# Two-layer transformer kernel: the causal mask of layer two's key-major scores moves from TensorE products to a VectorE minimum behind the exponentials, with a new order of all five engines

## What is computed

```python
xn = _layernorm(x, axis=-1)
x = x + _L1_attn_ref(xn, ...) + _L1_ffn_ref(xn, ...)      # 16 heads; 32 experts, top 6, and a shared expert

c = ...                                    # per head: keys in a latent of 64, normalised
scores = jnp.einsum('bhsl,bhtl->bhst', q_lat, c) * (1.0 / np.sqrt(L))
mask = jnp.tril(jnp.ones((Sx, Sx), dtype=bool))
scores = jnp.where(mask, scores, -jnp.inf)
w = jax.nn.softmax(scores, axis=-1)
oh = jnp.einsum('bhst,bhtd->bhsd', w, v)
```

## Time and profile before

| | |
|---|---|
| median of 3 runs | 2020.04 us (2015.65 to 2021.65) |
| profiled execution: device time | 2017.58 us |
| its span, first to last instruction | 2015.8 us |
| mean granted TensorE clock | 0.976 of full speed |
| TensorE busy | 1746.5 us, 87% |
| VectorE, GpSimd, ScalarE busy | 1100.9, 874.7, 819.5 us |
| one body, in the middle of the program | 116.2 us |

### The profile page before, as it was taken

One profiled execution on the slowest core, in us unless ns is written; L12 is line 12 of the kernel. 1 busy time (PEld: TensorE's weight loads), 2 busy tenths in 40 slices (PEclk: granted clock), 3 DMA queues, 4 the chain that ended last, 5 costly groups with the idle time before them and its releaser, 6 DMA issues.

```text
span 2015.8 us, 41842 instructions
## 1 busy us (share of the span) xinstructions
PE 1746.5 (87%) x16112; PEld 1333.6 (66%) x16112; DVE 1100.9 (55%) x2557; ACT 819.5 (41%) x1596; POOL 874.7 (43%) x995
## 2 busy tenths in 40 slices
PE   3657898989999998989989898999989899888887
PEld 2434676767677676767767676776767677675766
DVE  5645373655647365664737465473746547364442
ACT  2532435344343534334353433435353443534332
POOL 2312343535354454435444353534535353543455
PEclk7878999999999999999999999999999999999999
DMA  5632222313142231314132141413213141321221
GB/s 129 163 85 62 59 59 64 81 43 87 37 102 53 74 73 51 76 40 105 47 83 64 51 87 36 107 37 91 56 53 85 37 107 37 93 54 46 54 64 33
DMA packets 323318, 139.26 MB, mean 69 GB/s; under 512 B 227568, under 2 KB 308528, under 8 KB 323120
## 3 DMA queue, kind: packets, MB, share of 16 engines
q1 hardware_dynamic: 304688, 86.23, 18.5%
q0 software_dynamic: 18432, 50.36, 9.1%
HBM read 102.12 MB, written 29.88 MB: 65 GB/s over the span
## 4 chain that ended last, share of the span: by engine, by line
PE 26%; issue 25%; DVE 19%; POOL 17%; ACT 8%; SPq 3%; DMA 2%; POOLq 0%; DVEq 0%; ACTq 0%
PE s3r L1394 7%; POOL gs L762 6%; POOL h2l L771 5%; POOL cb L741 3%; PE s2acc L1391 3%; DVE th L1269 3%; DVE mx L1102 3%; PE s1a L1394 2%; DVE gs L1274 2%; PE s2r L1394 2%; PE s1acc L1497 2%; POOL h1p L706 2%; PE s1a L1514 2%; ACT h2h L967 1%; ACT p L876 1%
## 5 line engine op out<-in xcount | busy, mean ns | idle before, releaser
L771 POOL TENSOR_TENSOR h2l<-th,h2h 128x512 f16<-128x512 f32 (+1 forms) x224 | 246.5, 1103 | 390.9 <-ACT h2h L967 380.5
L762 POOL TENSOR_TENSOR gs<-gs,cb 128x512 f32<-128x512 f32 x192 | 243.9, 1270 | 263.6 <-DVE gs L1274 262.2
L967 ACT CAST h2h<-th 128x512 f16<-128x512 f32 (+1 forms) x224 | 131.2, 586 | 425.8 <-DVE th L1269 356.9
L1394 PE MATMUL s3r<-xe,xg 128*128 128x256 f16 x2304 | 284.5, 273 | 2.7 <-DVE gs L1274 2.7
L1391 PE MATMUL s2acc<-xd,h2h 128*128 128x256 f16 x1536 | 263.9, 274 | 24.5 <-POOL h2l L771 24.5
L1394 PE MATMUL s3r<-xe,xu 128*128 128x256 f16 x2304 | 283.0, 273 | 1.6 <-DVE th L1269 1.6
L1394 PEld LDWEIGHTS s3r<-xe,xg 128*128 128x128 f16 x2304 | 222.7, 98 | 39.9 <-DVE gs L1274 8.7
L1394 PEld LDWEIGHTS s3r<-xe,xu 128*128 128x128 f16 x2304 | 223.7, 98 | 31.6 <-DVE th L1269 5.5
L741 POOL DMA_DIRECT2D cb<-comb_d x384 | 229.0, 604 | 20.9 <-issue 11.2
L1274 DVE SCALAR_TENSOR_TENSOR gs<-th,s3r 128x512 f32<-128x512 f32 (+1 forms) x224 | 143.9, 642 | 148.8 <-ACT th L971 148.4
L1269 DVE TENSOR_TENSOR th<-s3r,gs 128x512 f32<-128x512 f32 x192 | 132.1, 688 | 168.5 <-POOL gs L762 164.5
(11 more groups left out here) (280 smaller groups left out, 3140.4 us busy)
## 6 DMA issues: line engine op xcount, KB each, us to landing
cb<-comb_d POOLq DMA_DIRECT2D x128, 192.0 KB, 3.4
part_d<-part SPq DMA_DIRECT2D x32, 512.0 KB, 3.3
cb<-comb_d POOLq DMA_DIRECT2D x128, 128.0 KB, 3.0
stacks<-part_d SPq DMA_DIRECT2D x192, 64.0 KB, 2.4
va<-v_d SPq DMA_DIRECT2D x512, 8.0 KB
cb<-comb_d POOLq DMA_DIRECT2D x128, 64.0 KB, 3.0
land<-part_d SPq DMA_DIRECT2D x96, 64.0 KB, 2.7
part<-part_d SPq DMA_DIRECT2D x96, 64.0 KB, 3.5
```

The source lines that it names most:

```text
L762: g.tensor_tensor(gc2[:, p % 2, :], gs2[:, p % 2, :], cb2[:, 2 * (p % 6):2 * (p % 6) + 2, :].rearrange("p a s -> p (a s)"), ALU.mult).then ...
L771: g.tensor_tensor(h2l[0:m, n % 2, 0:w], th2[0:m, n % 2, 0:w], h2h[0:m, n % 2, 0:w], ALU.subtract).then_inc(sem("h2l_made"), 1)
L967: s.copy(h2h[0:m, n % 2, 0:w], th2[0:m, n % 2, 0:w]).then_inc(sem("h2h_made"), 1)
L1394: ins = nc.tensor.matmul(bk, lhs[i][k], rhs[j][k], start=first, stop=last)
```

## The change

Three things:

1. The mask product of the key-major scores of layer two (old L1655, `mm(two(ring2[u % 2])[:, :, 0:P], identb, maskk1, ...)`) goes: 16 per sequence. The second score product of each head now ends the group and signals ScalarE. Entries above the diagonal go through the exponential unmasked.
2. VectorE gets one instruction per pair of heads (new L1242): a minimum, in place in p, of the two diagonal blocks of both heads (128 partitions by 4 x 128, fp32) with a table `keep1` (broadcast), which is 1e30 where the entry stays and 0 where it goes. It waits until the exponential of the pair's second head is done and signals `p2_masked`. `weigh` of four heads now waits for `p2_masked` of its second pair in place of the last exponential.
3. All 25 order strings are replaced (one each is shown).

```diff
@@ ORDERS @@
     "pe": {
-        "body": ("022020012122001121002101022221120220212100142212101012131301200103100101031101310120001003"
-                 "34300300403040003043343303001333133"),
+        "body": ("220020102010222101201021102241221022120202100121211112130132020101031100001100113033101003"
+                 "04300300403040003433041030333333031"),
...
@@
-        maskk1 = sb("maskk1", [P, P], BF16)
+        keep1 = sb("keep1", [P, P])
@@ def dve2 @@
+                dve.wait_ge(*emptied2(it, U2["k_rows", 2 * n + 1]))
+                diagonal = p1[:, :, :, :].rearrange("p s k (c q) -> p s (k c) q", q=P)[:, 2 * n % PSLOT:2 * n % PSLOT + 2, 0:3:2, :]
+                v.tensor_tensor(diagonal, diagonal, keep1[:, :].unsqueeze(1).unsqueeze(1).to_broadcast([P, 2, T, P]),
+                                ALU.min).then_inc(sem("p2_masked"), 1)
                 yield
@@
-            v.tensor_scalar(maskk1[:, :], mask_tmp[3], -BIG, None, ALU.add).then_inc(sem("dve_const"), 1)
+            v.tensor_copy(keep1[:, :], mask_tmp[3]).then_inc(sem("dve_const"), 1)
@@ def pe2, weigh @@
-                pe.wait_ge(*emptied2(it, U2["k_rows", QUAD * q + QUAD - 1]))
+                pe.wait_ge(*event("p2_masked", it, 2 * q + 2))
@@ def pe2 @@
-                        mm(ring2[u % 2][:, at:at + S - P * j], key(kst2, h, FULL)[:, P * j:P * j + P],
-                           query(qst2, h, FULL)[:, P * j:S], start=j == 0, stop=False, skip_group_check=True)
-                for u, h in pair:
-                    mm(two(ring2[u % 2])[:, :, 0:P], identb[:, :], maskk1[:, :].unsqueeze(1).to_broadcast([P, T, P]),
-                       start=False, stop=True, skip_group_check=True).then_inc(fills2(u), 1)
+                        ins = mm(ring2[u % 2][:, at:at + S - P * j], key(kst2, h, FULL)[:, P * j:P * j + P],
+                                 query(qst2, h, FULL)[:, P * j:S], start=j == 0, stop=j == T - 1, skip_group_check=True)
+                        if j == T - 1:
+                            ins.then_inc(fills2(u), 1)
```

More of the change, by code:

```diff
@@ new lines @@
+        "start": ("022200213010031120000002001213010300230101230000103112101410110020203034023111211143002020"
+                 "10234031010242341032330231133021231"),
+        "first": ("010002001310100113203211003032033223123101231131110023311212301023000103200043302100011110"
+                 "24040302400022012104214300322112000"),
+        "late": ("002001212110122011022201241112402221201221120002001312001203311321121002003301000040311300"
+                 "03110013003330433043043000330013031"),
@@ new lines @@
+        "start": ("001000020021003000110020200002020120121103011000413320113121230120131343031102333103211022"
+                 "24331020410101230104322012142333010"),
+        "first": ("104001002111022100312212300130100000020101011221301112012001133121311010213103202033231304"
+                 "20130022300401220400004300333343202"),
+        "late": ("202200120122200112110242120212140202221022121113121013003211030010320110103141031101030030"
+                 "10000300340030030040000103333413333"),
@@ new lines @@
+        "start": ("210002200110112010122010301000010000011222102000131030421100031032031234203332014340302010"
+                 "13212330000223124131023343321111010"),
+        "first": ("010011202021210010311020302001301000011112001232212213010310201111001231011323410331334001"
+                 "03002213202040000004300223323423034"),
+        "late": ("020210201212010212214201241202102022222114211011220132031301104320003011103101041311001300"
+                 "00030300030000030003100043133313333"),
@@ new lines @@
+        "start": ("220011201222000001003100010022111110102100120000102030001300310423214002213002240201400201"
+                 "31343101131023100322241313333313331"),
+        "first": ("120010100202121321000211102300030113132012120110000012210123001111113101321300402300123303"
+                 "41030002243020420021040033240303233"),
+        "late": ("002120010442212010202121201212142201111224222201031231100101313003011102103001312100013020"
+                 "01030003000300330000031433031033343"),
```

72 lines of the change are left out of this document (24 added, 48 removed), and 2 rows, old and new, of the table PER.

## The result

| | before | after |
|---|---|---|
| median | 2020.85 us (2015.65 to 2022.02, 4 runs) | 2099.74 us (2098.14 to 2104.04, 4 runs) |
| ratio to before, 95% interval | | 1.0398, 1.0381 to 1.0416 |
| one body, middle of the program | 116.21 us | 122.29 us |
| TensorE busy, whole program | 1746.5 us | 1753.0 us |
| mean granted TensorE clock | 0.976 | 0.959 |

The change costs 79 us, 4%. The prediction was 2008 us with a range to 2040: wrong in sign and 60 us outside the range.

A forecast was written before the change was run, and what follows sets the result against it. TensorE, busy 87% of the span, bounds the kernel. Per period -1.76 (masks) + 0 (A) + 1.4 (R) + 1.2 (P) - 1.4 (C) = -0.56 us, taken as -0.75, -12 us in all: 2008 us, range 1988 to 2040.

The forecast's parts named there:

- Nothing hides these products: Mask products: each pair costs TensorE's queue 0.22 us, 1.76 us per sequence, 28 us in all if idle time stays.
- rival 2: Nothing gained: the freed 1.76 us reappear as waits in R and P, set by SyncE and VectorE; 2014 to 2026 us, chance 0.18.
- The minimum, 0.65 us: VectorE: each of eight minima per sequence takes 0.65 us, 5.2 us per period, fitting into its idle time.
- the collision term: Minima on VectorE excluded by GpSimd instructions: 0.2 to 1 us per period, mostly in idle time, put at nothing.
- stretch A: Transpose of the maxima through key-major heads to the last value product's end: 23.74 us before, idle time forecast unchanged within 0.1.
- 0.9, 0.25 and 0.65 us: New waits in A from VectorE's queue, at the second and third value products and behind the first eight heads' normalising.
- C, "idle -1.4": Layer two's last value product to the Gram product, 56.03 us before: idle falls 1.4 us as down-product and output-product waits go.
- R, 23.2 us: Gram product to first query-major head, 22.14 us before: the DMA queue ends it, 23.2 us forecast, idle +1.4 us.
- 1.07 us: In R: two value loads of 0.535 us each ahead of the stack loads delay the first query-major head by this much.
- P, 12.9 us: First query-major head to the transpose of the maxima, 14.30 us before: VectorE bounds it, 12.9 us, idle +1.2 us.
- Rival 3: In A, value products each wait a whole minimum, 0.8 us: +1.3 us per period, 2041 us, chance 0.22.
- the faster cases: The forecast of part of the gain (2000 to 2014 us, 0.40) and the full gain (1992 us, 0.2), together 0.60.

The follow-up runs named there:

- filling products: Changed kernel with five products of 512 columns, results overwritten, put ahead of the third value product's wait for the minimum: 2077.66 us, ratio 1.0285.

## Why the prediction was wrong

**"Were all idle time unchanged, the time would fall by 28 us", and "Nothing hides these products".** The price of a pair, 0.22 us, is right, its credit is not. Removed alone, the masks bring 15 us in the old orders and 19 in the new ones: 0.79 and 0.99 us of 1.76 per period. The rest turns into longer waits for the exponentials, and in the old orders into a little of the lower clock. The prediction had the rows for it (1.11 and 0.64 us of waiting at the value products) and used them only as cover for the minimum; rival 2 had the mechanism, at other places.

**The minimum, 0.65 us and "hardly a longer one".** Alone 0.69 us, right. But 932 ns on average, three in a row 4.04 us. The step that failed is the collision term, 0.2 to 1 us per period "mostly in its idle time", put at nothing. Its count was not bad: "about one minimum in five", from GpSimd's busy share in the old stretch A (3.28 of 23.74 us), and 31 of 128 were long. But these are no random ones. They are the minima of pairs 5 and 6 (29 of the 31), each 1.07 us longer, 2.1 us per period, and TensorE waits for what both hold up. An average says nothing about engines that start from the same event: L1112 releases L719, and the minima are queued right behind L1112. The new GpSimd order also brings L748 and L771 into A, where GpSimd is now busy for 8.80 us. The rule was cited correctly and then priced at nothing. (The lower bound for a minimum, 0.41 us, fits no row that was shown; its own 1.15 ns per element gives 0.59. Nothing hangs on it.)

**The queue on VectorE, "0.9, 0.25 and 0.65 us".** The places were found: the second and third value product and the bank behind the normalising. Measured in the body at 1047.64: 0.87 us at the second value product (it waits for the exponential, and does so without any minimum), 1.05 at the third, 1.02 at pair 7, up to 1.66 in the period without the lower clock. The last two are four and one and a half times their terms, since both follow a minimum that GpSimd holds.

**The clock had no term.** The trace of before shows 1.00 in each stretch, so the prediction took products at the full clock as given. Idle time that moves together changes that: 1.7 us per period by the filling products (0.3 of it is there without the clock), and 1.8 us by two neighbouring periods of the changed kernel that differ in A alone (122.29 us with the lower clock, 120.54 without). So of the 4.2 us by which the last value product comes later than without any minimum (28.03 against 23.86), about 1.7 are the clock's, and the other 2.5, present in the period without the lower clock too (26.39), are the waits behind the minima.

**C, "idle -1.4".** Forecast C was 55.4 us (115.4 less the three others), 0.6 us shorter than before; cut at the same point in both kernels, it is 1.7 us longer (56.72 to 58.41), with and without a minimum. The walk credited waits that go and didn't see those that come: layer one's exponentials (0.78, 0.62) and its maximum (0.88) in C, and past the Gram product L909 (1.01) and L1273 (0.94) in R. The step that failed is to take the waits of the old order as the list of places where the new one can wait. Each product that is moved away from beside a chain lengthens the wait at that chain's end.

**R, 23.2 us.** 23.42 measured, but not for the reason given. The old SyncE order gave back 0.23 of the 1.07 us. R is longer because of the two waits just named; the DMAs are hidden beside them in half of the periods and end the stretch in the other half.

**P, 12.9 us.** 12.31: the VectorE-bound run is real (the wait for L1224 is 14.7 us in the program, 4.7 before), its 0.8 us for signals and refilling was too much. The sum was not right either: its terms behind the fourth pair add up to 8.1 us or more, not 7.9.

**The rivals.** Rival 3 named the right stretch and the right sign. Its price, 1.3 us per period, had a minimum's own length at each value product; at 2041 us it lay just outside the range that was said to reach it. Its chance of 0.22 was too small since its strongest "against", that VectorE is idle for more than half of A, is an average as well. VectorE was busy for 2.93 of the 3 us that mattered (1066 to 1069). And the faster cases rested on a sum of four stretches in which each term had the sign that the walk gave it; 41 us of the loss come from the orders with no minimum in the kernel.

## What to carry to other kernels

Work that is moved to an idle engine costs what stands behind it in that engine's queue, so ask for each moved instruction what else starts from the same event and who waits for the next entry; a busy share doesn't answer that, and nor does the name that a wait carries, since the delay can pass through a third engine. A product that stands ahead of an exponential which TensorE waits for is partly free: before crediting its removal, look whether the next wait simply grows. And a new order has to be priced chain by chain, by the TensorE work that stands beside each fixed chain, not by the waits that the old order happens to show.

## What the runs showed of the hardware

- **Idle TensorE time can be dearer than its length.** After 3 us in which TensorE was busy for 1.42, the granted clock was 0.50 for 6.8 us, and six products took 1.49 us in place of 0.84. Five products of no use in the gap (1.24 us) brought 22 us over the program.
- **A one-input minimum of 0.43 us meets GpSimd like the two-input one of 0.69**: up to 1.50 and 1.76 us beside the same additions, and the additions grow too (L719 from 1.27 to 1.65 us with the two-input minimum, to 1.38 with the other).
- **Two engines in lockstep**: while the queues of both are full, each instruction waits for one of the other. Moved apart, three minima took 1.89 us in place of 4.04.
